# Attention values computed by channels and turned back, score maxima put into the queries by VectorE, decays by one scan: a chain of four transformer layers on one core

## The chip, the cores and the metric

The kernel runs on one core of a Trainium2 chip. The metric is the device time of one launch in microseconds. PE is the matmul engine (TensorE), PEld its weight loads, DVE is VectorE, ACT is ScalarE, POOL is GpSimd, SP is the engine whose queue issues all DMA here.

## The reference

Thirty-two sequences of 128 tokens with 256 channels each pass through four layers, all in float32. Layer 0 adds one attention with 16 heads, whose result is the same for all sequences here and is computed once. Layer 1 is a state space block (convolution over time, gate, decaying state) and a cross attention with 8 heads. Layer 2 holds two attentions with 16 heads of 16 channels, the first causal, and a feed-forward part. Layer 3 holds one causal attention with 16 heads and a feed-forward part of 1024 channels.

```python
A = -jnp.exp(A_log)
decay = jnp.exp(dt * A)
dbx = dt[..., None] * xh
def step(h, inp):
    dec, u, bt, ct = inp
    h = h * dec[:, :, None, None] + u[..., None] * bt[:, None, None, :]
    y = jnp.einsum('bhpn,bn->bhp', h, ct)
    return (h, y)
...
score = jax.nn.softmax(energy / jnp.sqrt(jnp.asarray(dk, energy.dtype)), axis=-1)
out = jnp.einsum('bhst,bhtk->bhsk', score, V) * m
```

The state space block is computed without the loop over time: for each of its 8 heads a 128x128 matrix holds the product of all decays between two times, it is multiplied by the inner products of B and C, and one matmul with `dbx` gives y.

## The kernel before, in words

The work of one sequence is cut into some 70 tasks (`xhatT`, `Q2`, `quads2`, ...), and up to four sequences are in work at a time. There is no scheduler at run time: the tables `TASKS`, `FIRST`, `LAST`, `SETUP` and `SHIFT` give each task of each sequence a place, one sequence is 14 units after the one before, and every engine runs its tasks in the order of these places (`ORDER`). `SHIFT` gives an engine an order of its own for some tasks. Engines wait for one another by semaphores alone, and each works through its list strictly in order, so a task that has to wait holds up all behind it. `SPARE` names tasks of the first sequences ahead of which PE runs matmuls that nobody reads.

Results of matmuls pass through a ring of four banks of PSUM (`RING_BANKS`). `claim` waits until the bank's last user has been read, `filled` waits for the bank to be full, `evacuated` for it to be read. Four more banks (`score`) hold the scores.

An attention `a_` with 16 heads (0, 2, 3 and 4; there are 97 of them, three for each sequence and one in the setup) goes through these tasks:

- `quads` (L698): the scores with queries on the partitions; in causal attentions `lay_causal` (L662) first lays the mask down.
- `scores` on DVE (`maxima`, L1252): the negated maximum of each query and head, written to `maxima_at`.
- `mT` on PE (`turn_maxima`, `flip`, L618): the maxima are turned by two transposes. On ACT (`shifts`, L1053) they are copied to `shift_rows` in two scalings, and POOL (`shift`, L1585) adds these to the queries QB. Each head has spare channels among its 32, in which the keys KE hold a one, so the maximum enters through the matmul itself.
- `quadsT` (L722): the same scores with keys on the partitions, already less the maximum. `exps` on ACT (L1042) takes the exponentials into `weights`.
- `values` (L765): for each head and each block of 32 queries one matmul, the exponentials as 128x32 weights and V2 (16 channels and a column of ones, 17 columns) moving: 64 matmuls, each of them two instructions in float32 and as many weight loads. The four blocks of queries go to four groups of 32 columns of the engine.
- `finish` on DVE (`weighted`, L1263 and L1264): division by the sum, then the layer norm (`moments`, L1222 to L1218, a root on POOL, L1512, and `normalise_affine`, L1233 and L1235).

The decays: POOL (`log_decays`, `am`, L1558) makes a matrix of 128x1024 from the logarithms, `ld` on PE (L839) sums it by two matmuls with the triangle `after`, 512 columns each, ACT (`decays`, L1115) takes two exponentials, and `decayed` on DVE (L1377) multiplies by the inner products. `Y` on PE (L849) uses the result, the gate on DVE (`Y`, L1386 and L1388) follows.

Other lines that matter: L1342 is the convolution on DVE, L1397 the addition of the state space block's output to the residual, L1413 that of the cross attention's output (`Wo`), L1047 a copy of 128x512 from PSUM on ACT in the attention with 8 heads.

## Time and profile before

| | |
|---|---|
| median of the runs shown | 1811.0 us (3 runs, 1804.14 to 1812.05) |
| profiled execution | 1813.73 us, span 1811.9 us |
| PE busy | 1655.2 us (91%), 33980 matmul instructions and as many weight loads |
| DVE busy | 1341.2 us (74%) |
| ACT busy | 1096.6 us (61%) |
| POOL busy | 687.1 us (38%) |
| granted clock of PE, mean | 0.982 |

The busy times come from one execution. They are shares of the whole span; what a task is worth depends on who waits for it at its place. "issue" as releaser means that the engine waited for nothing the profile shows.

### The profile page before, as it was taken

How to read it: one execution, taken by the hardware profiler on the slowest of the kernel's cores; microseconds unless marked ns; L12 is line 12 of the kernel's file. 1: busy time of each engine (PE TensorE's matmuls, PEld its weight loads, DVE VectorE, ACT ScalarE, POOL GpSimd, SP SyncE). 2: the span in 40 equal slices, each digit the busy share in tenths (PEclk: the TensorE clock that was granted, in tenths of full speed). 3: DMA queues.
4: the chain of work that ended last, by engine and by line, in shares of the span. 5: the costliest groups of instructions: out<-in, count | busy, mean ns of one | idle time of the engine just before them, and what ended most of it. 6: DMA issues, size and time to landing. Idle time of an engine off the chain costs nothing.

```text
span 1811.9 us, 78837 instructions
## 1 busy us (share of the span) xinstructions
PE 1655.2 (91%) x33980; PEld 1415.6 (78%) x33980; DVE 1341.2 (74%) x3357; ACT 1096.6 (61%) x2796; POOL 687.1 (38%) x1384
## 2 busy tenths in 40 slices
PE   6799989999999999999999999989999999999986
PEld 6678878787778777888787888877788777778765
DVE  4578867787867777867787877778777777787652
ACT  2456665575565665566565666656566656566653
POOL 2444433444423444433444433344333344443320
PEclk9999999999999999999999999999999999999998
DMA  7000000000000000000000000000000000000000
GB/s 262 12 6 3 11 14 12 11 3 11 9 14 11 12 3 11 12 12 12 11 3 11 12 12 11 12 6 9 11 12 12 12 12 3 12 9 5 6 3 10
DMA packets 26264, 28.71 MB, mean 16 GB/s; under 512 B 2240, under 2 KB 25024, under 8 KB 25792
## 3 DMA queue, kind: packets, MB, share of 16 engines
q1 hardware_dynamic: 25920, 23.67, 4.0%
q8 instruction: 271, 4.44, 1.0%
q14 instruction: 73, 0.60, 0.1%
HBM read 19.47 MB, written 4.19 MB: 13 GB/s over the span
## 4 chain that ended last, share of the span: by engine, by line
PE 71%; DVE 18%; issue 7%; ACT 2%; POOL 2%; DVEq 0%; DMA 0%; SPq 0%; POOLq 0%; ACTq 0%
PE ring L630 22%; PE ring L636 16%; PE ring L618 7%; PE ring L765 7%; DVE conv L1342 6%; PE score L698 6%; PE score L722 4%; PE ring L839 3%; PE score L662 2%; PE ring L849 2%; DVE maxima_at L1252 2%; DVE conv L1337 1%; PE ring L741 1%; POOL stat L1512 1%; PE score L678 1%
## 5 line engine op out<-in xcount | busy, mean ns | idle before, releaser
L1009 ACT COPY actT<-ring 128x256 f32<-128x256 f32 x256 | 94.4, 377 | 322.2 <-PE ring L618 322.1
L1252 DVE TENSOR_REDUCE maxima_at<-score 128x4 f32<-128x512 f32 x388 | 240.5, 681 | 56.3 <-PE score L698 56.2
L1512 POOL TENSOR_TENSOR stat<-stat 128x1 f32<-128x1 f32 x224 | 135.7, 610 | 376.7 <-DVE stat L1218 374.9
L1585 POOL TENSOR_TENSOR QB<-QB,shift_rows 128x512 f32<-128x512 f32 x97 | 124.5, 1283 | 288.5 <-ACT shift_rows L1053 288.4
L1042 ACT ACTIVATE weights<-score 128x512 f32<-128x512 f32 x388 | 200.3, 606 | 16.2 <-PE score L722 15.8
L1342 DVE SCALAR_TENSOR_TENSOR conv<-raw,vectors,conv 128x128 f32<-128x128 f32 x576 | 197.0, 397 | 6.8
L765 PE MATMUL ring<-V,weights 128*32 128x17 f32 x12416 | 131.4, 186 | 47.4 <-issue 46.0
L765 PEld LDWEIGHTS ring<-V,weights 128*32 128x32 f32 x12416 | 118.8, 110 | 62.9 <-issue 52.5
L630 PE MATMUL ring<-actT,w_q 128*128 128x128 f32 x1024 | 143.0, 282 | 10.8 <-issue 8.9
L630 PEld LDWEIGHTS ring<-actT,w_q 128*128 128x128 f32 x1024 | 124.9, 192 | 13.6 <-issue 8.4
L1526 POOL TENSOR_TENSOR dts<-dts,row_all 128x8 f32<-128x8 f32 x32 | 6.9, 216 | 323.7 <-ACT dts L1103 323.7
L630 PE MATMUL ring<-actT,w_up 128*128 128x128 f32 x1024 | 127.7, 278 | 0.5 <-ACT actT L1009 0.5
L722 PE MATMUL score<-QB,KE 32*128 32x128 f32 x3104 | 117.2, 287 | 5.7 <-POOL QB L1585 3.2
L630 PEld LDWEIGHTS ring<-actT,w_up 128*128 128x128 f32 x1024 | 119.3, 192 | 3.5 <-ACT actT L1009 0.7
L636 PE MATMUL ring<-w_down,gT 128*128 128x256 f32 x512 | 120.0, 388 | 2.1 <-issue 2.1
L722 PEld LDWEIGHTS score<-QB,KE 32*128 32x128 f32 x3104 | 98.0, 189 | 26.6 <-issue 19.4
L1235 DVE SCALAR_TENSOR_TENSOR res<-att,stat,row_all 128x256 f32<-128x256 f32 x128 | 75.0, 586 | 47.8 <-POOL stat L1512 46.3
L636 PEld LDWEIGHTS ring<-w_down,gT 128*128 128x128 f32 x512 | 97.5, 196 | 16.3 <-issue 3.6
L630 PE MATMUL ring<-cT,w_k 128*128 128x128 f32 x768 | 104.8, 279 | 0.0
L1233 DVE SCALAR_TENSOR_TENSOR att<-res,stat,row_all 128x256 f32<-128x256 f32 x128 | 102.5, 801 | 0.0
L630 PEld LDWEIGHTS ring<-cT,w_k 128*128 128x128 f32 x768 | 95.5, 191 | 5.5
L636 PE MATMUL ring<-w_v,cT 128*128 128x256 f32 x384 | 99.3, 381 | 0.3 <-issue 0.3
(174 smaller groups left out, 3955.2 us busy)
## 6 DMA issues: line engine op xcount, KB each, us to landing
cT<-in_ctxT SPq DMA_DIRECT2D x32, 128.0 KB, 2.3
x_in<-in_x SPq DMA_DIRECT2D x32, 128.0 KB, 2.3
out<-result SPq DMA_DIRECT2D x32, 128.0 KB, 1.7
row_all<-in_rows SPq DMA_DIRECT2D x1, 1420.0 KB, 9.9
w_in<-in_in_proj SPq DMA_DIRECT2D x1, 1288.0 KB, 7.1
w_k<-in_k SPq DMA_DIRECT2D x4, 256.0 KB, 6.6
w_v<-in_v SPq DMA_DIRECT2D x4, 256.0 KB, 6.3
w_q<-in_q SPq DMA_DIRECT2D x4, 256.0 KB, 7.3
```

The costliest lines, as they stand in the source:

```text
L618: last = nc.tensor.transpose(t[:, c * P:(c + 1) * P], src[:, c * P:(c + 1) * P], ident)
L630: last = mm(t[:, at:at + P], w[:, c, cols:cols + P], xT[:, c, :], start=(c == 0), stop=(c == n - 1))
L636: last = mm(t[:, at:at + hi - lo], xT[:, c, :], w[:, c, lo:hi], start=(c == 0), stop=(c == n - 1))
L698: last = mm(score[:, r, at:at + P], QB[rows_of, l, c, e, :], keys, start=(not masked and at == 0), stop=(c == DC - 1 and f == 1))
L722: last = mm(score[:, r, at:at + P], KE[rows_of, l, c, e, :], QB[rows_of, l, c, e, :], start=(not masked and at == 0), stop=(c == DC - 1 an ...
L765: last = mm(output[queries, h * (DH16 + 1):(h + 1) * (DH16 + 1)], weights[:, buffer, r, at + queries.start:at + queries.stop], V2[:, l, h, :],
L1042: run(weights[:, turned_buffer(it, a_, l), r, :], score[:, r, :], ACT.Exp).then_inc(S["exps"], 1)
L1233: step(stt(att[:, l, :], res[:, l, :], stat[:, l, 0:1], rows[g], ALU.subtract, ALU.mult))
L1252: nc.vector.tensor_reduce(maxima_at[:, maxima_buffer(it, a_, l), :, 32 * r:32 * r + 17:16], score[:, r, :].rearrange("p (c f k) -> p c f k ...
L1342: last = stt(conv[:, l % 2, c, :], raw[:, l % 2, c, k:k + P], conv_w[:, c, k:k + 1], conv[:, l % 2, c, :], ALU.mult, ALU.add)
L1512: tt(stat[:, l, 10:11], stat[:, l, 2:3], stat[:, l, 4:5], ALU.pow).then_inc(S[done], 1)
L1585: tt(QB[:, l, :, :, :], QB[:, l, :, :, :], shift_rows[:, :, :, :], ALU.add).then_inc(S[f"shift{a_}"], 1)
```

## The change

It does four things.

1. Values by channels. V2 is widened from 17 to 32 columns (the rest is zero) and becomes the weights, 128x32, one matmul for each head; the exponentials move, 128 queries at a time. The result has channels on the partitions. ACT copies it to `attT` (task `attT`), PE turns it back by four transposes (new task `back`, three more ring jobs for each sequence), and DVE reads `weighted` from the turned bank.
2. Maxima. `shift_rows`, ACT's scalings and POOL's addition go. DVE (`shifted`, in the task `mT`) multiplies the turned maxima in PSUM by `spare_row` and adds them to QB in two instructions.
3. Decays. POOL's 128x1024 product and the two matmuls go. PE turns the 128x8 logarithms (one transpose, one ring job instead of two), ACT takes the exponential of 8x127 into `rates_row`, SP writes these rows to DRAM (`ld`) and reads them back into all 128 partitions (`spread`, 4 KB each). DVE runs one `tensor_tensor_scan` over 128x1024 against `delta`, which holds the identity for each head, and `decayed` follows.
4. Orders. The tables of places are new for all engines, and so are the spare matmuls (113 instead of 63).

In the steady part the new order of PE is the following, with the number of the sequence relative to the one that enters; the old order differs from it by one to three places for most tasks and has no `back`, and DVE runs `scan` and `decayed` between `norm3` and `scores2`:

```
xhatT[0] Q1[-1] row[-2] xbc0[0] x3T[-2] mT4[-3] quads1[-1] K3[-2] Q3[-2] z1[0] xbc1[0] quads3[-2] turn1[-1] V3[-2] e3[-2] values1[-1]
n3[-2] quadsT4[-3] ctxT[-1] V1[0] Wo[-1] mT3[-2] z0[0] values4[-3] x2T[-1] ld[0] quadsT3[-2] pairs[0] back4[-3] K2[-1] values3[-2] Q2[-1]
back3[-2] K4[-2] V4[-2] x6T[-3] e2[-1] quads2[-1] V2[-1] x4T[-2] up0[-3] fc1[-2] Y[0] up1[-3] mT2[-1] fc2[-2] uT[0] quadsT2[-1] n2[-1]
proj[0] K1[0] x5T[-2] values2[-1] Q4[-2] xnT[0] back2[-1] down[-3] quads4[-2]
```

The core of the diff, the tables of places left out:

```diff
+def att_buffer(it, a_, l):
+
+    return it.number(TURNED_AT, a_, l) % ATT_BUFFERS
+
...
-        V2 = sb("V2", [P, G, H16, DH16 + 1])
+        V2 = sb("V2", [P, G, H16, P // TILES])
...
-        shift_rows = sb("shift_rows", [P, DC, 2, P])
+        attT = sb("attT", [P, ATT_BUFFERS, 4 * P])
...
+            def ld(it, l):
+                b, use = job(it, "ld", l)
+                sp.wait_ge(bank_read[b], use + 1)
+                sp.dma_start(rates_out[l % 2], rates_row[:, l % 2, :]).then_inc(S[f"rates_out{l % 2}"], 16)
+
+            def spread(it, l):
+                sp.wait_ge(S[f"rates_out{l % 2}"], nth_of_two(it, l) * 16)
+                sp.dma_start(decay[:, l % 2, :, :], rates_out[l % 2].partition_broadcast(P)).then_inc(S[f"decay_in{l % 2}"], 16)
+
...
-                pe.wait_ge(S[f"shift{a_}"], 1 if a_ == 0 else nth(it, l))
+                evacuated(it, f"mT{a_}", l)
...
                 buffer = turned_buffer(it, a_, l)
-                for c in range(DC):
+                for four in range(H16 // TILES):
                     for r in range(TILES):
-                        for e in range(2):
-                            h, at = 8 * c + 2 * r + e, (2 * c + e) * P
-                            for q, queries in enumerate(ROWS_OF):
-                                last = mm(output[queries, h * (DH16 + 1):(h + 1) * (DH16 + 1)],
-                                          weights[:, buffer, r, at + queries.start:at + queries.stop], V2[:, l, h, :],
-                                          start=True, stop=True)
-                                if h == H16 - 1:
-                                    last.then_inc(full if q == TILES - 1 else S[f"att_full{q}"], 1)
+                        h = TILES * four + r
+                        at = (2 * (h // 8) + h % 2) * P
+                        last = mm(output[ROWS_OF[r], four * P:(four + 1) * P], V2[:, l, h, :],
+                                  weights[:, buffer, h % 8 // 2, at:at + P], start=True, stop=True)
+                        if four == H16 // TILES - 1:
+                            last.then_inc(full if r == TILES - 1 else S[f"att_full{r}"], 1)
+
+            def back(it, a_, l):
+                evacuated(it, f"values{a_}", l, (f"back{a_}", l))
+                flip(it, f"back{a_}", l, attT[:, att_buffer(it, a_, l), :], 4)
 
             pe.wait_ge(S["const_in"], 16)
...
 
             def ld(it, l):
                 pe.wait_ge(S["am"], nth(it, l))
-                for half in range(2):
-                    t, full = claim(it, f"ld{half}", l)
-                    mm(t[:, :], after, decay[:, l % 2, 4 * half:4 * half + 4, :].rearrange("p h k -> p (h k)"),
-                       start=True, stop=True).then_inc(full, 1)
+                t, full = claim(it, "ld", l)
+                nc.tensor.transpose(t[0:MH, 0:P], dts[:, 5, l, :], ident).then_inc(full, 1)
...
 
-            def shifts(it, a_, l):
-
-                t, read = filled(it, f"mT{a_}", l)
-                for e in range(2):
-                    last = run(shift_rows[:, :, e, :], t[:, 0:D].rearrange("p (c k) -> p c k", c=DC), ACT.Copy,
-                               scale=spare_row[:, e:e + 1])
-                last.then_inc(read, 1)
+            def out_turned(it, a_, l):
+                for r in range(TILES - 1):
+                    act.wait_ge(S[f"att_full{r}"], nth_output(it, a_, l))
+                t, read = filled(it, f"values{a_}", l)
+                nc.scalar.copy(attT[:, att_buffer(it, a_, l), :], t[:, :]).then_inc(read, 1)
 
             def extended_keys(it, a_, l):
...
             def decays(it, l):
-                for half in range(2):
-                    t, read = filled(it, f"ld{half}", l)
-                    run(decay[:, l % 2, 4 * half:4 * half + 4, :].rearrange("p h k -> p (h k)"), t[:, :],
-                        ACT.Exp).then_inc(read, 1)
+                t, read = filled(it, "ld", l)
+                run(rates_row[:, l % 2, 1:], t[0:MH, 1:P], ACT.Exp).then_inc(read, 1)
 
             def Y(it, l):
...
+            def shifted(it, a_, l):
+
+                if a_ in (2, 3):
+                    dve.wait_ge(S[f"q{a_}_first"], nth(it, l))
+                t, read = filled(it, f"mT{a_}", l)
+                for e in range(2):
+                    last = stt(QB[:, l, :, e, :], t[:, 0:D].rearrange("p (c k) -> p c k", c=DC), spare_row[:, e:e + 1],
+                               QB[:, l, :, e, :], ALU.mult, ALU.add)
+                last.then_inc(read, 1)
+
             def weighted(it, a_, l, step, dst):
 
-                for r in range(TILES - 1):
-                    dve.wait_ge(S[f"att_full{r}"], nth_output(it, a_, l))
-                t, read = filled(it, f"values{a_}", l)
-                o = t[:, 0:H16 * (DH16 + 1)].rearrange("p (h e) -> p h e", h=H16)
+                t, read = filled(it, f"back{a_}", l)
+                o = t[:, :].rearrange("p (h e) -> p h e", h=H16)
                 step(nc.vector.reciprocal(rec[:, l, :], o[:, :, DH16]))
                 tt(dst.rearrange("p (h e) -> p h e", h=H16), o[:, :, 0:DH16],
                    rec[:, l, :].unsqueeze(2).broadcast_to((P, H16, DH16)), ALU.mult).then_inc(read, 1)
-                evacuated(it, f"values{a_}", l)
+                evacuated(it, f"back{a_}", l)
 
             def x1(it, l):
...
+            nc.vector.tensor_copy(delta[:, :].rearrange("p (h k) -> p h k", h=MH), ident.unsqueeze(1).broadcast_to((P, MH, P)))
+            nc.vector.memset(rates_row[:, :, :], 0.0)
             nc.vector.memset(maxima_at[:, :, :, :], 0.0).then_inc(S["ready_consts"], 1)
...
+                def scan(l):
+                    dve.wait_ge(S[f"decay_in{l % 2}"], nth_of_two(it, l) * 16)
+                    across = decay[:, l % 2, :, :].rearrange("p h k -> p (h k)")
+                    step(nc.vector.tensor_tensor_scan(across, across, delta[:, :], 0.0, ALU.mult, ALU.add))
+
                 def decayed(l):
-                    jobs = sorted(("CB", "ld1"), key=lambda what: place(it, what, l))
-                    for what in {job(it, what, l)[0]: what for what in jobs}.values():
-                        evacuated(it, what, l)
+                    evacuated(it, "CB", l)
                     tt(decay[:, l % 2, :, :], decay[:, l % 2, :, :],
                        state_gate[:, l % 2, :].unsqueeze(1).broadcast_to((P, MH, P)), ALU.mult).then_inc(S["M"], 1)
...
+            nc.gpsimd.memset(V2[:, :, :, DH16 + 1:], 0.0).then_inc(S["ones_col"], 1)
...
-                    step(tt(dts[:, 5, l, :], dts[:, 10, l, :], decay_rate, ALU.mult))
-                    tt(decay[:, l % 2, :, :], before.unsqueeze(1).broadcast_to((P, MH, P)),
-                       dts[:, 5, l, :].unsqueeze(2).broadcast_to((P, MH, P)), ALU.mult).then_inc(S["am"], 1)
+                    tt(dts[:, 5, l, :], dts[:, 10, l, :], decay_rate, ALU.mult).then_inc(S["am"], 1)
 
...
-
-                def shift(a_, l):
-
-                    evacuated(it, f"mT{a_}", l)
-                    tt(QB[:, l, :, :, :], QB[:, l, :, :, :], shift_rows[:, :, :, :], ALU.add).then_inc(S[f"shift{a_}"], 1)
 
                 def norm5(l):
```

## Rows read from the trace of the kernel before

**Rows 1.** The page: busy time and share, and the chain that ended last.

```profile
PE 1655.2 (91%) x33980; PEld 1415.6 (78%) x33980; DVE 1341.2 (74%) x3357; ACT 1096.6 (61%) x2796; POOL 687.1 (38%) x1384
...
PE 71%; DVE 18%; issue 7%; ACT 2%; POOL 2%; DVEq 0%; DMA 0%; SPq 0%; POOLq 0%; ACTq 0%
```

**Rows 2.** Stretch 200 to 1600 us: length, busy PE, PEld, DVE, ACT, POOL, clock, DMA share, GB/s.

```profile
200.00:1600.00 1400.00, 1305.99 (x27230) 1120.54 (x27229) 1081.37 (x2688) 878.89 (x2243) 556.87 (x1113) 0.99 0.04 10
```

**Rows 3.** Line 839: durations min/median/max, first and last start.

```profile
L839 PEld LDWEIGHTS ring<-decay,const x128: 186/190/338, 45.8 to 1681.7; 128*128 128x128 f32 x128
```

**Rows 4.** PE's waits from 200 to 1600 us: total, times, longest.

```profile
PE ring L765 <- issue: 34.1, 29, 2.1
PE ring L618 <- DVE res L1413: 19.0, 23, 0.9
...
PE ring L636 <- issue: 1.1, 2, 0.8
```

**Rows 5.** Timeline of PE: start, length, what, idle before.

```profile
812.99 1.25 PE L765 MATMUL ring<-V,weights 128*32 128x17 f32 x127
815.40 0.18 PE L765 MATMUL ring<-V,weights 128*32 128x17 f32 x1 [1.16 <-issue]
...
816.73 0.60 PE L618 MATMUL ring<-const,conv 128*128 128x128 f32 x4
817.16 1.06 PE L630 MATMUL ring<-actT,w_k 128*128 128x128 f32 x8
...
823.20 1.88 PE L839 MATMUL ring<-decay,const 128*128 128x512 f32 x4
824.92 1.03 PE L636 MATMUL ring<-w_v,cT 128*128 128x256 f32 x4
...
829.63 1.10 PE L849 MATMUL ring<-dbx,decay 128*32 128x64 f32 x64
...
834.42 1.17 PE L722 MATMUL score<-QB,KE 32*128 32x128 f32 x32
...
838.83 1.27 PE L765 MATMUL ring<-V,weights 128*32 128x17 f32 x128
840.03 1.16 PE L630 MATMUL ring<-actT,w_q 128*128 128x128 f32 x8
```

**Rows 6.** The page: PE's instruction queue and two DMA issues, us to landing.

```profile
q8 instruction: 271, 4.44, 1.0%
...
x_in<-in_x SPq DMA_DIRECT2D x32, 128.0 KB, 2.3
...
row_all<-in_rows SPq DMA_DIRECT2D x1, 1420.0 KB, 9.9
```

**Rows 7.** Groups by shape: busy us, mean ns, idle before.

```profile
L1585 POOL TENSOR_TENSOR QB<-QB,shift_rows 128x512 f32<-128x512 f32 x97 | 124.5, 1283 | 288.5 <-ACT shift_rows L1053 288.4
...
L1233 DVE SCALAR_TENSOR_TENSOR att<-res,stat,row_all 128x256 f32<-128x256 f32 x128 | 102.5, 801 | 0.0
...
L1377 DVE TENSOR_TENSOR decay<-decay,state_gate 128x1024 f32<-128x1024 f32 x32 | 38.7, 1210 | 2.7 <-ACT decay L1115 2.6
...
L1047 ACT COPY weights<-ring 128x512 f32<-128x512 f32 x64 | 34.4, 590 | 19.5 <-PE ring L618 19.5
...
L1397 DVE SCALAR_TENSOR_TENSOR res<-ring,stat,res 128x256 f32<-128x256 f32 x32 | 15.5, 484 | 13.3 <-PE ring L636 11.2 <-POOL stat L1512 1.2
```

**Rows 8.** Lines 1233 and 1388: duration ns min/median/max.

```profile
L1233 DVE SCALAR_TENSOR_TENSOR att<-res,stat,row_all x128: 473/476/2054, 94.0 to 1796.2; 128x256 f32<-128x256 f32 x128
...
L1388 DVE TENSOR_TENSOR zs<-tz,zs x32: 691/1030/1540, 52.2 to 1689.1; 128x512 f32<-128x512 f32 x32
```

**Rows 9.** Timeline of DVE and of POOL at the decays' product.

```profile
819.06 2.05 DVE L1233 SCALAR_TENSOR_TENSOR att<-res,stat,row_all 128x256 f32<-128x256 f32 x1
...
818.94 1.90 POOL L1558 TENSOR_TENSOR decay<-const,dts 128x1024 f32<-128x1024 f32 x1
```

**Rows 10.** DVE's waits from 200 to 1600 us.

```profile
DVE res L1235 <- POOL stat L1512: 37.4, 73, 0.9
```

More of the change, by code:

```diff
@@ L224 @@
 MAXIMA_BUFFERS = 2
+ATT_BUFFERS = 2
 RING_BANKS = 4
@@ L347 @@
 down norm3; norm5 x1r"""
[L348 to L352 removed]
+NEXT_BUT_ONE = "Y ld; pairs xbc0; proj z1; Y z1; Y pairs; uT pairs; Y dt; decayed pairs; down up0; store down; x1 loadx; proj xbc0; uT xbc0"
+DVE_ALONE = ("finish2 norm2 finish3 norm3 norm4 finish4 norm5 x1 x1r xhat spread scan decayed conv0 conv1 silu loadx loadc").split()
 def in_time(chains, later):
```

352 lines of the change are left out of this document (171 added, 181 removed).

## Prediction

> **What bounds the kernel now.** I read the page first, then the stretches, one line's first and last start, PE's waits, two pieces of the timeline, and the groups by shape. PE is busy 91% of the span, DVE 74%, ACT 61%, POOL 38%; the chain that ended last runs 71% on PE, 18% on DVE and 7% through "issue", time in which the engine waited for nothing the profile shows [rows 1]. The clock is at its upper level (2.4 GHz) nearly throughout, granted 0.99 from 200 to 1600 us [rows 2], so everything is costed at that level. The decay matmuls start first at 45.8 and last at 1681.7 us [rows 3]; 31 steps lie between, so one sequence takes 52.8 us. The 1400 us from 200 to 1600 hold 26.5 sequences: PE busy 1305.99/26.5 = 49.2 us each, DVE 1081.37/26.5 = 40.8 us [rows 2].
>
> What PE waits for there is the main reading. Seven "issue" rows, from 34.1 down to 1.1 us, add to 71.6 us (2.7 us a sequence); the rows with DVE as releaser, nearly all of it the 19.0 us behind Wo, to 20.9 us (0.8 us) [rows 4]. With the 1306.0 us busy that fills the 1400. The largest issue row belongs to the value products, and the stall sits inside them: 1.16 us after 127 of 128 instructions [rows 5]. `values` waits at its start only, so no semaphore can stop it there. It puts out 128 matmul instructions with 128 weight loads in 1.20 us (838.83 to 840.03 [rows 5]), while PE's instruction queue brought 4.44 MB in 271 packets [rows 6], 16.4 KB each: one for some 251 of PE's 67,960 matmuls and weight loads. I take the stalls for instructions that come too late where PE uses up a whole packet in about 1.2 us.
>
> **The change, part by part, for one sequence.**
>
> Decays on PE. Removed: four instructions of 512 columns, 823.20 to 824.92 = 1.72 us. Added: one transpose, 0.43/4 = 0.11 us (four took 816.73 to 817.16) [rows 5]. Together -1.61 us.
>
> Values, three times. Before 1.20 us each; a row of the timeline is 0.07 longer than the distance to the next start, since it holds the tail of its last matmul (1.27 against 1.20), and I take that off the others. After: 32 matmul instructions in 8 rounds of four side by side, 128 columns each. No row shows 128x32 weights with 128 columns. A round of four takes 37.5 ns at 17 columns (1.20 us/32) and 64 ns at 64 (L849, 1.03 us/16 [rows 5]); along that slope 128 columns give 100 ns. Weights of 32 rows and 128 columns with the same 128 columns moving take 137 ns (L722, 1.10 us/8 [rows 5]). So 0.80 to 1.10 us; nearer the rows with the same weights, I take 0.95: -0.25 each, -0.75 us.
>
> Turning back, three times four transposes at 0.43 us: +1.29 us. PE work in all: 49.2 - 1.61 - 0.75 + 1.29 = 48.1 us (47.7 to 48.6).
>
> Stalls. A value product falls from 128 to 32 matmul instructions, and no other group of PE's puts out so many so fast: L849 has 64 in 1.03 us [rows 5]. I leave 0.2 of the 2.7 us: -2.5 us (0 to -2.7). One page speaks against this step. The Trainium skill, "Runtime: NRT & Kernel Launch", section "Instruction fetch mechanics", says that an engine's instruction memory is refilled in 16 KiB blocks while the current one is executed, and that this is mostly hidden. By that rule the 2.7 us have another cause and may stay. The packet size in this trace agrees with the page; a stall in the middle of a group without a wait doesn't agree with "hidden".
>
> DVE. Added: six updates of QB. The nearest row is L1397, also a scalar_tensor_tensor of 128x256 with one input in PSUM, 484 ns [rows 7]: 2.9 us. Added: one scan of 128x1024. No row shows a scan. Below stands one pass over as much, L1377, 1.21 us [rows 7]; above, two such passes, one for the multiply and one for the add, 2.42 us. I take 2.4, since each element needs the one before it. The Trainium skill, "DVE: opcode table, instruction layouts, handler registers and perf-mode slots", section "Datapath and trigger behaviour", says that this scan runs at half throughput; from the length of L1377 that would be 2.4 us too, and no run here shows it yet.
>
> DVE also gets time back. L1233 takes 476 ns in the median but 801 on average, up to 2054 [rows 7, 8]: at 819.06 it lasted 2.05 us beside POOL's product for the decays (818.94, 1.90 us [rows 9]). The excess is 128 x 0.325 = 41.6 us; that of L1388, median over minimum, 32 x 0.34 = 11 us [rows 8]. Both large partners on POOL go: that product and the update of QB (L1585, 1.28 us, 97 times [rows 7]). With some 8 us at the convolution, an estimate, 61 us or 1.9 us a sequence; bounds 0 and 2.5. DVE then: 40.8 + 2.9 + 2.4 - 1.9 = 44.2 us.
>
> ACT loses two exponentials and six scalings and gains three copies of 128x512 at 0.59 us (L1047 [rows 7]) and one small exponential; at 878.89/26.5 = 33 us [rows 2] it has room. The copy lies behind `values`; `back` comes one or two tasks later, about 1 us of PE work, so only tenths show. Ahead of the transposed scores, two ACT scalings and 1.28 us of POOL become 2 x 0.48 us on DVE, but in DVE's queue: in front of `mT3` there stands half a convolution, in front of `mT2` the state space layer's gate. `quadsT` waits for it, and behind `quadsT` all of PE.
>
> The trip through DRAM. In the new order eleven PE tasks from quadsT3 to e2 stand between `ld` and where DVE comes to the scan, by their rows' lengths 7.6 us. The trip is an exponential (0.3, an estimate), a write and a spread of 512 KB; the rows are 2.3 us for 128 KB and, for a broadcast, 9.9 us for 1420 KB while all weights shared the queues [rows 6]. With 2 and 3 us the trip is 5.3 us: hidden. On SP's queue `spread` stands behind loadc of the next sequence, an old store and a loadx; what these wait for ended a period earlier, and they cost their issue.
>
> How DVE and PE meet. DVE needs its 44.2 us, the POOL roots and ACT sums it waits for (37.4 us in the largest row [rows 10], with two smaller ones 67.3 us, 2.5 a sequence) and some 1.4 of small gaps: 48.1 us, as much as PE. Scan and `decayed` (3.6 us) lie between `norm3` and `Y`, while PE has up0 and fc1 (3.1 us); then comes the gate, then `mT2`. I expect half a microsecond there and 1.0 elsewhere: PE's waits for DVE go from 0.8 to 2.2 us (0.8 to 4).
>
> Sum: 48.1 + 0.2 + 2.2 = 50.5 against 52.8, -2.3 us, times 31 = -71. Start: the trip and the scan less POOL's product, +4. End: no stalls, but two turns back, -2. The order of tasks is otherwise nearly the old one. In all -69: span 1811.9 to 1743. The profiled run took 1813.7, 1.8 more than its span and 0.15% over the median of 1811.0 of the runs shown; 1743 + 1.8 = 1744.8, less 0.15%: 1742. I say 1740.
>
> **Rivals.**
> - The stalls stay: what stops PE isn't the value products' own pace. They would then hide DVE's waits: 48.1 + 2.7 + 0.8 = 51.6, -1.2 x 31 = -37, with start and end 1776. For it speaks that under half of the issue time carries the value products' line; against it, where they stand. The rule of the skill's page above leads here.
> - DVE becomes the bound. Today it idles 12.0 us a sequence, 8 of them for PE; if half of that can't be taken out of two interlocked queues, 48.1 + 4.0 = 52.1: -0.7 x 31 = -22, 1791. For it speaks that both engines now need 48.1 us.
> - All goes in, DVE's waits stay 0.8 and no stall is left: 48.9, -3.9 x 31 = -121, 1692.
> - Slower: the spread is late. At 9.9 us, and 2.3 for the write, the trip is 12.5 us against 7.6 of cover; 4.9 us a sequence stop DVE at the scan, with scores2, Y and mT2 queued behind: 48.1 + 0.2 + 0.8 + 4.9 = 54.0, +1.2 x 31 = +37, about 1850. It decides from a trip of 7.6 + 3.6 = 11.2 us. Against it: in the steady stretch the DMA engines are busy 4% [rows 2].
>
> That the change does nothing is no case: instructions fall away.
>
> **Numbers.** Chances: the forecast 0.50 (its own range 1712 to 1768), stalls stay 0.12, DVE bound 0.17, all in 0.13, spread late 0.06, something not seen 0.02. The range 1700 to 1792 leaves out the last two and half of "all in" and of little else. Half a per cent, 9 us, is about what a measurement of this kernel can tell from no change. Faster 0.88, same 0.04 (the upper edge of the DVE case), slower 0.08.
>
> **What the changed profile would show.** Value products: 3104 matmul instructions, 0.95 x 97 = 92 us of PE and under 110 busy; issue rows of 200 to 1600 us under 10 us (near 70, and the first rival is right). L1233's counterpart at a mean near 480 ns, DVE at 83% of its span, the scan at 1.2 to 2.4 us. A wait of DVE for the spread in the steady stretch would be the last rival. PE's waits for DVE near 2 us a sequence, at the transposed scores and at Y; each microsecond more or less there moves the time by 31, and that is what would make the prediction wrong first.

## The result: 1672 us, faster than forecast

The changed kernel takes 1672.27 us (median of 4 runs, 1670.92 to 1675.6) against 1808.24 us (4 runs on the same chip). The ratio is 0.9251, 95% interval [0.9223, 0.9279]. I had forecast 1740 with a range of 1700 to 1792: the sign is right, the size is not, and the time lies below the range, beyond even the rival "all goes in" (1692).

The page of the changed kernel: busy times, the chain that ended last by engine, PE's instruction queue, and the new transfer through DRAM (KB each, us to landing). They answer to [rows 1, 6].

```profile
PE 1616.5 (97%) x25060; PEld 1393.2 (83%) x25060; DVE 1387.1 (83%) x3585; ACT 1039.8 (62%) x2667; POOL 493.3 (29%) x1256
...
PE 55%; DVE 36%; issue 5%; POOL 2%; DMA 1%; ACT 1%; SPq 0%; DVEq 0%; POOLq 0%; ACTq 0%
...
q8 instruction: 202, 3.31, 0.8%
...
decay<-rates_out SPq DMA_DIRECT2D x32, 512.0 KB, 3.9
```

PE is busy 97% of the span in place of 91%, and DVE's share of the chain has doubled: both engines are now close to the whole period. The stretch 200 to 1500 us (columns as in [rows 2]), the line of the Y products with its first and last start (durations in ns first), and the three largest of PE's five waits in that stretch (total us, times, longest):

```profile
200.00:1500.00 1300.00, 1291.56 (x20548) 1118.15 (x20547) 1140.52 (x2944) 856.64 (x2201) 408.82 (x1042) 1.00 0.07 21
```

```profile
L858 PE MATMUL ring<-dbx,decay x2048: 216/219/243, 50.3 to 1546.7; 128*32 128x64 f32 x187
```

```profile
PE ring L858 <- DVE decay L1396: 3.9, 22, 0.4
PE ring L843 <- DVE conv L1364: 1.2, 4, 0.4
PE ring L849 <- POOL dts L1578: 0.5, 2, 0.3
```

Y starts 31 steps apart from first to last: (1546.7 - 50.3)/31 = 48.27 us for a sequence, where [rows 3] gave 52.8. I use this period for every kernel below. The 1300 us hold 1300/48.27 = 26.9 sequences. PE is busy 1291.56/26.9 = 48.0 us in each and idle 0.31 (8.4 us in 1300), of which the three rows above and the two others, 0.5 and 0.3 us, make 6.4. In the stretch no "issue" row of PE is left, where [rows 4] had 34.1 us at one line and 71.6 in all (in 1400 us). DVE is busy 1140.52/26.9 = 42.35 us.

Two pieces of PE's timeline (start, length, what, idle before):

```profile
810.30 1.10 PE L858 MATMUL ring<-dbx,decay 128*32 128x64 f32 x64 [0.16 <-DVE decay L1396]
...
819.36 1.08 PE L773 MATMUL ring<-weights,V 128*32 128x128 f32 x32
820.37 1.16 PE L639 MATMUL ring<-actT,w_q 128*128 128x128 f32 x8
```

The value products take 820.37 - 819.36 = 1.01 us without a gap, against 1.20 plus stalls in [rows 5]. Y, which I took for a place where PE waits, waits 0.16 us. The groups by shape that answer to [rows 7, 8], and the new ones (busy us, mean ns, idle before):

```profile
L1358 DVE SCALAR_TENSOR_TENSOR conv<-raw,vectors,conv 128x128 f32<-128x128 f32 x576 | 169.0, 349 | 6.8
L1269 DVE SCALAR_TENSOR_TENSOR QB<-ring,const,QB 128x256 f32<-128x256 f32 x194 | 84.5, 477 | 20.4 <-PE ring L627 20.3
L1392 DVE TENSOR_TENSOR_SCAN decay<-decay,delta 128x1024 f32<-128x1024 f32 x32 | 73.1, 2284 | 3.0 <-DMA decay<-rates_out 3.0
...
L1241 DVE SCALAR_TENSOR_TENSOR res<-att,stat,row_all 128x256 f32<-128x256 f32 x128 | 62.3, 487 | 39.6 <-POOL stat L1533 36.3 <-DVE att L1239 0.4
L1239 DVE SCALAR_TENSOR_TENSOR att<-res,stat,row_all 128x256 f32<-128x256 f32 x128 | 60.9, 476 | 0.0
...
L1407 DVE TENSOR_TENSOR zs<-tz,zs 128x512 f32<-128x512 f32 x32 | 22.1, 692 | 1.1
```

L1239 is the old L1233: 476 ns on average, not 801. L1407 is the old L1388: 692, not 1056. DVE waits 3.0 us in the whole run for the spread row, so the trip through DRAM is hidden.

### The profile page after: what moved, and what is told of

The parts are those of the page before. It is cut to its first block, busy times and chain, and to the rows that moved or that the text cites. A ratio compares the mean times of both kernels' runs of the same rounds, so it can differ in the third digit from the quotient of the medians.

```text
span 1673.8 us, 61139 instructions
## 1 busy us (share of the span) xinstructions
PE 1616.5 (97%) x25060; PEld 1393.2 (83%) x25060; DVE 1387.1 (83%) x3585; ACT 1039.8 (62%) x2667; POOL 493.3 (29%) x1256
## 4 chain that ended last, share of the span: by engine, by line
PE 55%; DVE 36%; issue 5%; POOL 2%; DMA 1%; ACT 1%; SPq 0%; DVEq 0%; POOLq 0%; ACTq 0%
PE ring L639 18%; PE ring L645 14%; PE ring L627 6%; DVE conv L1358 5%; DVE maxima_at L1258 5%; PE score L707 4%; DVE decay L1392 4%; PE score L731 3%; PE ring L773 3%; DVE decay L1396 2%; PE ring L858 2%; DVE conv L1364 2%; DVE QB L1269 2%; DVE conv L1353 2%; PE score L671 2%
## 5 line engine op out<-in xcount | busy, mean ns | idle before, releaser
L1533 POOL TENSOR_TENSOR stat<-stat 128x1 f32<-128x1 f32 x224 | 131.7, 594 | 617.2 <-DVE stat L1224 616.6
L1358 DVE SCALAR_TENSOR_TENSOR conv<-raw,vectors,conv 128x128 f32<-128x128 f32 x576 | 169.0, 349 | 6.8
L1184 ACT ACTIVATE gT<-ring,vectors 128x128 f32<-128x128 f32 x256 | 73.0, 368 | 72.2 <-PE ring L639 71.5
L645 PE MATMUL ring<-w_down,gT 128*128 128x256 f32 x512 | 115.9, 379 | 1.3 <-issue 1.3
L773 PE MATMUL ring<-weights,V 128*32 128x128 f32 x3104 | 106.9, 278 | 3.4 <-issue 3.3
L1269 DVE SCALAR_TENSOR_TENSOR QB<-ring,const,QB 128x256 f32<-128x256 f32 x194 | 84.5, 477 | 20.4 <-PE ring L627 20.3
L1063 ACT COPY attT<-ring 128x512 f32<-128x512 f32 x97 | 56.2, 579 | 72.7 <-PE ring L773 72.6
L773 PEld LDWEIGHTS ring<-weights,V 128*32 128x32 f32 x3104 | 80.5, 111 | 23.8 <-issue 10.1
L639 PE MATMUL ring<-actT,w_in 128*128 128x128 f32 x768 | 98.7, 279 | 0.7 <-DVE q_bias L1337 0.7
```

Source lines behind the costliest of these rows:

```text
L639: last = mm(t[:, at:at + P], w[:, c, cols:cols + P], xT[:, c, :], start=(c == 0), stop=(c == n - 1))
L645: last = mm(t[:, at:at + hi - lo], xT[:, c, :], w[:, c, lo:hi], start=(c == 0), stop=(c == n - 1))
L773: last = mm(output[ROWS_OF[r], four * P:(four + 1) * P], V2[:, l, h, :], weights[:, buffer, h % 8 // 2, at:at + P], start=True, stop=True)
L1184: last = run(gT[:, l % 2, c, :], t[:, k * P:(k + 1) * P], ACT.Gelu, bias=up_b[:, c:c + 1])
L1269: last = stt(QB[:, l, :, e, :], t[:, 0:D].rearrange("p (c k) -> p c k", c=DC), spare_row[:, e:e + 1], QB[:, l, :, e, :], ALU.mult, ALU.add)
L1358: last = stt(conv[:, l % 2, c, :], raw[:, l % 2, c, k:k + P], conv_w[:, c, k:k + 1], conv[:, l % 2, c, :], ALU.mult, ALU.add)
```

## Experiments

All twelve have the kernel before beside them on the same chip; its median moved between 1807 and 1819 us. The changed kernel was measured only for the result, where the kernel before had 1808, so a difference from its 1672 us can be off by some us, by about 10 in run 12. Line numbers shift by a few lines between the kernels.

**1 and 2. Computation and order apart.** The change does two things at once: it computes three parts otherwise, and it has new orders of tasks for all engines. The first kernel has the old computation under the new orders, the second the new computation under the old ones. Tasks that the borrowed order doesn't have were put in by hand, next to their producers.

```diff
 the first (the second has it the other way round, with the new computation):
-    K1=-101.6778, K2=-85.3719, K3=-77.8105, K4=-66.1055, KE2=-53.2043, KE3=-34.7422, Q1=-92.624, Q2=-86.0387, Q3=-77.5392,
+    K1=27.1941, K2=36.4796, K3=45.2686, K4=51.2561, KE2=36.4927, KE3=55.6023, Q1=30.3419, Q2=36.7225, Q3=45.6768, Q4=56.4087,
...
```

> All three parts of the computation as before (values by queries, maxima through ACT and POOL, decays by POOL's product and two matmuls), under the new orders; finish4 a little earlier on DVE, and the last exps4 a little later on ACT, so that nothing blocks. Instruction theory (the stalls of PE come from the value products' 128 matmul instructions, the rest of the gain from less work): the orders alone are worth little, 1780 to 1815 us, and the issue rows of PE from 200 to 1500 us stay above 50 us. Rival, the orders made the gain: below 1750 us and the issue rows under 20 us.

> The changed computation under the old tables of places; the new tasks get places next to their neighbours (back half a unit to one unit after values, scan just ahead of decayed). Theory that DVE has slack once its collisions with POOL and PE's stalls are gone: one sequence takes 48.5 to 49.5 us, 1680 to 1715 us in all. Rival, as I had forecast: DVE and PE block each other at 48 us of need each and only a tuned order avoids it: 50.5 us and more a sequence, 1740 us and above, with PE's waits for DVE above 2 us a sequence.

Measured: 2033.86 us (ratio 1.1274 [1.1204, 1.1344]) and 2094.68 us (1.1577 [1.1534, 1.1619]). The first is far from both expectations, in its "issue" rows too (33.9 us from 200 to 1500, where the theory wanted over 50 and the rival under 20); the second lies on the rival's side and far beyond its figure. PE's largest waits from 200 to 1600 us, of the first:

```profile
PE score L669 <- POOL QB L1592: 95.0, 24, 4.0
PE ring L846 <- POOL decay L1565: 28.1, 16, 2.4
PE ring L772 <- issue: 26.5, 29, 2.4
```

and of the second:

```profile
PE ring L644 <- DVE V L1482: 75.1, 16, 5.7
PE ring L632 <- ACT attT L1068: 36.7, 46, 3.5
PE ring L632 <- DVE res L1437: 26.3, 19, 1.4
```

What is to be seen: in the first, PE stands 4 us at the transposed scores in each sequence until POOL has added the shift to the queries; with these tasks placed as they are, the new order leaves no room for ScalarE's copies and that addition. In the second, PE waits for results that DVE makes in time in the order meant for it. PE's busy time for the same instructions grew too: 52.3 us a sequence against 49.3 in the kernel before, and 52.0 against 48.0 in the changed one; the granted clock of the stretch is 0.94 in both runs, against 0.99 and 1.00. An order and a computation belong together, and neither half can be read as the share of its part. The hand-placed tasks are untuned, so the 224 and 285 us above the kernel before say only that much.

**3. The value products alone put back** (queries on the rows of the result, 128 matmul instructions of 17 columns, no turning back):

```diff
-                        last = mm(output[ROWS_OF[r], four * P:(four + 1) * P], V2[:, l, h, :],
-                                  weights[:, buffer, h % 8 // 2, at:at + P], start=True, stop=True)
+                            for q, queries in enumerate(ROWS_OF):
+                                last = mm(output[queries, h * (DH16 + 1):(h + 1) * (DH16 + 1)],
+                                          weights[:, buffer, r, at + queries.start:at + queries.stop], V2[:, l, h, 0:DH16 + 1],
+                                          start=True, stop=True)
```

> The changed kernel with only the value products as before: 128 matmul instructions each of 17 columns, no copy to attT, no turning back (finish4 a little earlier on DVE). PE's work falls by 3 x (1.01 + 0.44 - 1.20) = 0.75 us a sequence. Instruction theory: the stalls come back, 2 to 2.7 us a sequence, inside or just behind the value products, which gives 1710 to 1735 us. Rival, the stalls had another cause (order, ring of banks, ACT): no stalls, 47.5 us a sequence, about 1650 us.

Measured: 1801.77 us (0.9963 [0.9939, 0.9987]), period (1670.5 - 49.6)/31 = 52.3 us, 4.0 more than the changed kernel's. PE's waits from 200 to 1600 us:

```profile
PE ring L840 <- DVE conv L1355: 40.6, 19, 3.2
PE ring L773 <- issue: 22.2, 13, 2.6
PE score L730 <- issue: 9.6, 8, 1.9
```

The "issue" rows are back (38 us in all), at the value products and at work behind them. A wait for DVE that the changed kernel hardly has (1.2 us) is now the largest. The time is far above the expected 1710 to 1735 us, and not because of the stalls: the "issue" rows make 1.4 us a sequence, less than the 2 to 2.7 expected. PE's waits for DVE make 1.8 us, 1.6 more than in the changed kernel, and its busy time is 49.0 us a sequence instead of the 47.2 that the work alone would give; the granted clock is 0.96 against 1.00.

**4. Instruction supply by itself.** PE alone, no waits: 24 times 64 products of 17 columns, 32 of 64, 16 of 128, and 64 of 17 again (its last part is as the first). Each product is two matmul instructions in the trace, with a weight load each. It computes nothing of the reference.

```
for bank, (count, columns) in enumerate(((64, 17), (32, 64), (16, 128), (64, 17))):
    for _ in range(24):
        for n in range(count):
            q = slice(32 * (n % 4), 32 * (n % 4) + 32)
            last = mm(ring[bank][q, 0:columns], w[:, q], w[:, 0:columns], start=True, stop=True)
```

> PE alone, no waits, zero operands; the output is zeros and nothing of the reference is computed. 24 times each: 128 matmul instructions of 17 columns (as the value products before), 64 of 64 columns (as Y), 32 of 128 columns (as the value products after), then the first again. Instruction theory: the first and the last part can't hold 1.20 us a product; they run on average at 1.6 us or more with pauses that name no releaser, the part with 32 instructions holds about 1.0 us without pauses. Rival, supply is no limit: all parts hold 1.20, 1.03 and 1.0 us a product without pauses.

One run, span 257.5 us. PE's timeline, two pieces of the first part and one of the third:

```profile
9.74 1.91 PE L42 MATMUL ring<-w 128*32 128x17 f32 x128 [1.55 <-issue]
...
13.20 1.91 PE L42 MATMUL ring<-w 128*32 128x17 f32 x128 [1.55 <-issue]
...
135.96 10.68 PE L42 MATMUL ring<-w 128*32 128x128 f32 x384 [0.46 <-issue]
```

Exactly 128 matmul instructions with their 128 weight loads, then a pause with no releaser, and again: the next 128 start 3.45 to 4.0 us after the last. Nothing in the kernel could hold them up. The page has PE's instruction queue at 65 packets for 16,896 matmuls and weight loads, one for 260. With 64 columns the pauses are still there (0.5 to 2.0 us). With 128 columns, 384 matmul instructions take 10.68 us, 3.6 for 128, and the pauses all but vanish. So the instruction theory holds: in this kernel PE gets 256 instructions in about 3.6 us and no faster. The granted clock was 1.00 from 9 to 90 us and 0.50 from 180 to 250, and lots, lengths and pauses are the same in both. A lot of the first part takes 1.91 us where the full kernel needs 1.20; why is not shown, but one lot of 17 columns right behind the part with 128 took 1.26 us, and the next still started 3.73 us after it.

**5 and 6. The maxima alone, the decays alone put back,** under the orders of the changed kernel (with places given by hand to the tasks that come back).

```diff
-                    last = stt(QB[:, l, :, e, :], t[:, 0:D].rearrange("p (c k) -> p c k", c=DC), spare_row[:, e:e + 1],
-                               QB[:, l, :, e, :], ALU.mult, ALU.add)
+                    last = run(shift_rows[:, :, e, :], t[:, 0:D].rearrange("p (c k) -> p c k", c=DC), ACT.Copy,
+                               scale=spare_row[:, e:e + 1])
...
+                    tt(QB[:, l, :, :, :], QB[:, l, :, :, :], shift_rows[:, :, :, :], ALU.add).then_inc(S[f"shift{a_}"], 1)
```

```diff
-                nc.tensor.transpose(t[0:MH, 0:P], dts[:, 5, l, :], ident).then_inc(full, 1)
+                    mm(t[:, :], after, decay[:, l % 2, 4 * half:4 * half + 4, :].rearrange("p h k -> p (h k)"),
+                       start=True, stop=True).then_inc(full, 1)
...
-                    step(nc.vector.tensor_tensor_scan(across, across, delta[:, :], 0.0, ALU.mult, ALU.add))
...
+                    tt(decay[:, l % 2, :, :], before.unsqueeze(1).broadcast_to((P, MH, P)),
+                       dts[:, 5, l, :].unsqueeze(2).broadcast_to((P, MH, P)), ALU.mult).then_inc(S["am"], 1)
```

> The changed kernel, with the maxima alone put back: ScalarE makes the scaled copies of mT, GpSimd adds them to the queries, VectorE does none of it. Per sequence VectorE loses about 2.9 us of work, GpSimd gets about 5, ScalarE about 2.6, TensorE's work is the same. Theory A (VectorE's load was what I priced wrongly; PE waits when VectorE is full): the time stays at 1672 or falls a little, 1660 to 1680. Theory B (what counts is how long the results are under way in an order that leaves them little room: two engines in place of one between mT and quadsT): PE waits for GpSimd's addition, some 2 to 3.5 us in each sequence as in the first run, 1730 to 1790.

> The changed kernel, with the decays alone put back: GpSimd multiplies, two products of 512 columns, ScalarE's exponential over 1024 columns; no scan, no way through DRAM. TensorE gets 1.6 us more for each sequence, VectorE loses the scan of 2.3. Theory A (work alone, since PE is busy 97% of the span and VectorE gets freer): 1672 + 32 x 1.6 = 1724, 1710 to 1735. Theory B (the way from the decay rate to Y is a chain of its own, and the product on GpSimd comes late in this order, as the 28.1 us in the first run): 1745 to 1790.

Measured: 1940.65 us (1.0719 [1.0676, 1.0763]) with a period of 56.5 us, and 1810.68 us (0.9992 [0.9965, 1.0018]) with one of 52.5. PE's waits from 200 to 1500 us, of the maxima's run and of the decays':

```profile
PE score L672 <- POOL QB L1603: 87.1, 22, 4.0
PE score L732 <- POOL QB L1603: 23.9, 23, 2.5
```

```profile
PE ring L848 <- POOL decay L1576: 40.7, 22, 2.3
```

In both runs DVE has less to do than in the changed kernel (40.3 and 41.7 us a sequence), and the time is longer: theory B of both, but beyond its 1790, by 21 us with the decays and by 151 with the maxima. Per sequence PE waits 111/23.0 = 4.8 us for POOL's addition there. PE's busy time grows too, to 1172.09/23.0 = 51.0 us from 48.0, for the same instructions; the granted clock of the stretch is 0.94 against 1.00, after waits of up to 4 us. With the decays, the period is 4.3 us longer: PE idles 1.6 us more, and its busy time is 2.7 us longer, not the 1.6 expected (the matmuls of 512 columns took 762 ns on average, 645 in the kernel before). The decays' run also shows in its groups and its timelines what DVE and POOL do to each other:

```profile
L1364 DVE SCALAR_TENSOR_TENSOR conv<-raw,conv 128x768 f32<-128x768 f32 x25 | 59.0, 2359 | 0.9
```

```profile
808.76 2.44 DVE L1364 SCALAR_TENSOR_TENSOR conv<-raw,conv 128x768 f32<-128x768 f32 x1
```

```profile
808.50 1.90 POOL L1576 TENSOR_TENSOR decay<-const,dts 128x1024 f32<-128x1024 f32 x1
```

The silu product takes 2359 ns on average beside POOL's product, and 1135 over the same stretch of the changed kernel. It began 0.26 us after POOL's and ended 0.80 us after POOL's end (808.76 + 2.44 against 808.50 + 1.90): most of it was done only when POOL had finished. The Trainium skill, "SBUF — State Buffer", section "SBUF: two separate sides", says that a VectorE instruction with two SBUF inputs and a GpSimd one that reads SBUF exclude each other for the whole instruction. The trace agrees nearly: by that rule it would have waited POOL's remaining 1.64 us and then taken its own 1.14, 2.8 us in all, and it took 2.44.

**7 and 8. What a microsecond of DVE costs.** The changed kernel with dummy reductions: two of 128x1024 behind the scan, or four of 128x512 at K1, both halves of the convolution, and the scan.

```diff
                     step(nc.vector.tensor_tensor_scan(across, across, delta[:, :], 0.0, ALU.mult, ALU.add))
+                    for j in range(2):
+                        step(nc.vector.tensor_reduce(spill[:, 0:1], across, AX_X, ALU.max))
```

> The changed kernel with two more VectorE reductions over 128x1024 behind each scan, whose result nobody reads: about 2.4 us more for each sequence, 42.4 + 2.4 = 44.8, a little over the 44.2 that I had forecast for VectorE, and that on the way from the scan to Y. Theory A (PE's waits go by VectorE's load): the 2.2 us of waits that I forecast come back, 1672 + 60 = 1730, 1715 to 1745. Theory C (VectorE's 5.9 us of idle time in each sequence takes it): at most 1685. If the place counts and not the load, PE's wait for the decays L1396 grows to some 2 us in each sequence, 1720 to 1750.

> The changed kernel with four more VectorE reductions over 128x512 for each sequence, one behind K1, one behind each half of the convolution and one behind the scan, whose result nobody reads: about 2.5 us more, as much as in the run before this one, but in four places. Theory A (load): the same as there, 1715 to 1745. Theory C (slack): at most 1685. The place counts: clearly less than there, 1680 to 1705.

Measured: 1768.44 us (0.9783 [0.9732, 0.9833]), period (1637.5 - 50.8)/31 = 51.2, and 1739.23 us (0.9609 [0.9572, 0.9647]), period (1613.0 - 51.2)/31 = 50.4. The added groups' rows, of the first and of the second:

```profile
L1395 DVE TENSOR_REDUCE spill<-decay 128x1 f32<-128x1024 f32 x50 | 61.0, 1220 | 1.7
```

```profile
L1363 DVE TENSOR_REDUCE spill<-delta 128x1 f32<-128x512 bf16 x52 | 35.1, 676 | 0.0
L1396 DVE TENSOR_REDUCE spill<-delta 128x1 f32<-128x512 bf16 x25 | 17.2, 686 | 0.9
L1349 DVE TENSOR_REDUCE spill<-delta 128x1 f32<-128x512 bf16 x25 | 16.9, 676 | 0.0
```

and PE's waits:

```profile
PE ring L859 <- DVE decay L1399: 63.5, 24, 2.8
```

```profile
PE ring L859 <- DVE decay L1400: 21.0, 24, 1.2
PE ring L628 <- DVE res L1436: 16.1, 22, 1.1
PE ring L917 <- DVE nonzero L1446: 14.7, 26, 1.1
PE ring L844 <- DVE conv L1367: 7.2, 21, 0.7
```

At the scan, 2 x 1.22 = 2.44 us make the period 2.9 longer; in four places, 2.7 us make it 2.1 longer. DVE has 5.9 us idle in each sequence of the changed kernel, and little of it takes the work. Theory C is out; run 8 lies in theory A's range, run 7 lies 23 us above it. The idle time is in small pieces (at most 0.8 us each in the timeline of one period that I read, mostly at POOL's roots and at PE's transposes), and each piece is there because the next input isn't; that this is why work put in front of it is not made up is my reading of these rows. The place changes the price from 0.8 to 1.2 us of time for a microsecond of DVE.

**9 and 12. The old instruction count in the new form.** Each value product of 128 columns is cut into four of 32, with the same result: 128 matmul instructions and 128 weight loads for a layer. In run 9 four neighbours write the same group of 32 rows, from the same weights loaded anew; in run 12 (the loop over `part` outside the one over `r`) they go round the four groups.

```diff
-                        last = mm(output[ROWS_OF[r], four * P:(four + 1) * P], V2[:, l, h, :],
-                                  weights[:, buffer, h % 8 // 2, at:at + P], start=True, stop=True)
+                        for part in range(4):
+                            last = mm(output[ROWS_OF[r], four * P + part * 32:four * P + part * 32 + 32], V2[:, l, h, :],
+                                      weights[:, buffer, h % 8 // 2, at + part * 32:at + part * 32 + 32], start=True, stop=True)
```

> The changed kernel, computing the same, with each value product of 128 columns cut into four of 32 over the same weights: 128 products with 128 weight loads for a layer of attention instead of 32 and 32, which is the instruction count of the old value products; columns, results and all the rest as they are. Instruction theory (the old stalls came from the count alone): pauses without a releaser come back on TensorE, some 2.5 us in each sequence, and 0.2 us more work for a layer, 0.6 in a sequence: 1672 + 32 x 3.1 = 1771, and some more where the order knocks on, 1745 to 1800. Rival (the stalls came from something else in the old form, its narrow writes or who read them): no pauses, only the work, 1675 to 1700.

> As the run with the value products in quarters, but the four quarters go round the four groups of 32 rows of the result, one after the other, as the old value products did; in the run before four neighbours wrote the same group, and a layer's 128 products took 2.7 us in place of the 1.2 that I had counted on. 128 products of 33 columns that go round took 13 ns each in the trace of before (19.8 us for 1536), so 1.65 us for a layer here, 0.6 more than the changed kernel's, 1.9 in a sequence: 1672 + 61 = 1733. Instruction theory: pauses without a releaser on TensorE again, more than the 1.4 us for each sequence of the run before since the products go faster, 2 to 3 us, so 1800 to 1840. Rival: no pauses worth naming, 1725 to 1750.

Measured: 1887.68 us (1.0436 [1.0402, 1.0469]), period 54.5, and 1820.34 us (1.0019 [0.9988, 1.0051]), period (1685.7 - 51.9)/31 = 52.7. The timeline of PE, of run 9:

```profile
825.39 2.74 PE L774 MATMUL ring<-weights,V 128*32 128x32 f32 x128
828.06 0.44 PE L627 MATMUL ring<-const,res 128*128 128x128 f32 x2
```

and of run 12, and under it run 12's waits of PE from 200 to 1500 us:

```profile
837.99 1.13 PE L774 MATMUL ring<-weights,V 128*32 128x32 f32 x108
841.10 0.38 PE L774 MATMUL ring<-weights,V 128*32 128x32 f32 x20 [1.99 <-issue]
...
864.79 1.30 PE L774 MATMUL ring<-weights,V 128*32 128x32 f32 x128
866.02 0.44 PE L627 MATMUL ring<-const,res 128*128 128x128 f32 x2
```

```profile
PE ring L774 <- issue: 48.1, 20, 3.7
PE ring L639 <- issue: 9.5, 5, 3.0
PE score L731 <- issue: 5.2, 6, 1.2
PE ring L627 <- issue: 3.8, 4, 2.4
```

Run 12 does a layer's values in 1.23 us (864.79 to 866.02), nearly the 1.20 of the old form, and the pauses are back in the middle of a group, as in [rows 5]: 66.8 us in 1300/52.7 = 24.7 sequences, 2.7 us in each, the very figure of before. Order of tasks, data and columns are the changed kernel's; only the products were cut into more instructions. The period is 4.4 us longer: 2.5 us are idle time, 0.7 the value products (3 x 0.22), and the other 1.3 are busy time of PE outside them, at a granted clock of 0.98 against 1.00. The time falls into the expected range partly by luck, since the products were much faster than the 1.65 us that I had put. Run 9's products are slower (2.67 us a layer), and its pauses smaller, 1.4 us a sequence (34.1 us of such rows in 23.8 sequences): the slower PE went through its instructions, the less it waited for them. My expectation for run 9 had the work wrong, 0.2 us more for a layer where it was 1.66: I had not reckoned with what four neighbours in one group of rows cost. Whether it is the shared group of rows or the shared weights that makes them slower, these two runs don't separate.

**10. DVE without the scan.** The spread row goes into the gate as it is, so the decays are not computed.

```diff
-                    step(nc.vector.tensor_tensor_scan(across, across, delta[:, :], 0.0, ALU.mult, ALU.add))
```

> The changed kernel without the scan of the decays (the spread row goes into the gate as it is, so its output isn't the reference's): VectorE loses 2.28 us for each sequence, 42.4 to 40.1, all else the same. If VectorE's load goes on deciding below where it stands, as it did when I added to it (27 to 39 us for each us in a sequence), 1672 - 60 = 1610. If TensorE alone is the bound now (it waits 0.31 us in a sequence), no more than these waits: 1660 to 1672.

Measured: 1661.78 us (0.9193 [0.9167, 0.922]), period (1535.5 - 46.3)/31 = 48.04. DVE's 2.28 us less are worth 0.23 us of the period, less than the 0.31 that PE had been idle; the first Y comes 4.0 us earlier. PE is busy 1294.12 of the 1300 us, so from here on it sets the time.

**11. More for POOL.** Two products of 128x512 from two SBUF inputs behind the decay rate; nobody reads them.

```diff
+                    for j in range(2):
+                        step(tt(spill[:, :, :], ident.unsqueeze(1).broadcast_to((P, 4, P)),
+                                gate_mask.unsqueeze(1).broadcast_to((P, 4, P)), ALU.mult))
```

> The changed kernel with two more GpSimd products of 128x512 from two inputs behind the decay rate, whose result nobody reads: about 2.5 us more for each sequence on an engine that is busy 29% of the span. If only VectorE's own load counts: 1672 to 1680. If GpSimd's work slows VectorE's instructions beside it (in the run with the decays put back, the silu product took 2.36 us instead of 1.14 beside GpSimd's): 1 to 1.3 us more on VectorE in a sequence, and at 27 to 39 us for each us, 1700 to 1725; the rows of VectorE's silu or convolution are then longer.

Measured: 1719.09 us (0.9508 [0.9475, 0.954]), period (1591.5 - 51.7)/31 = 49.7, 1.4 more. DVE's groups by shape over the span, and under them two waits from 200 to 1500 us:

```profile
L1240 DVE SCALAR_TENSOR_TENSOR att<-res,stat,row_all 128x256 f32<-128x256 f32 x128 | 85.6, 669 | 0.0
...
L1365 DVE SCALAR_TENSOR_TENSOR conv<-raw,conv 128x768 f32<-128x768 f32 x32 | 53.6, 1674 | 5.4 <-ACT raw L1119 4.3
```

```profile
PE ring L844 <- DVE conv L1365: 17.5, 26, 0.9
```

```profile
DVE res L1242 <- POOL stat L1534: 27.8, 54, 0.7
```

Not one instruction was added to DVE, but its busy time grew: by 85.6 - 60.9 = 24.7 us at the norm, 53.6 - 36.4 = 17.2 at the silu (36.4 in the changed kernel) and 4.1 at the convolution, 46.0 us, 1.4 a sequence. The period grew by the same 1.4. A busier POOL could also have delayed its results; DVE's largest wait for it didn't grow (27.8 us, 28.0 in the changed kernel), and PE's waits for it are 0.2 us a sequence.

## Why the prediction was right and wrong

**Right: PE's work.** 48.1 us forecast, 48.0 measured. Inside it the values took 1.01 us a layer where I had 0.95 in a range of 0.80 to 1.10, and a turn back takes 0.44 (821.58 to 822.02) where I had 0.43. With these the sum would be 48.3; the granted clock of the stretch, 1.00 against 0.99, may be the rest.

**Right: the stalls are instructions that come late.** 0.2 us forecast to be left, none seen. Runs 4, 9 and 12 show it apart from the rest: with nothing but more instructions for the same columns, 2.7 us a sequence come back. The first rival (the stalls stay) is out. The Trainium skill, "Runtime: NRT & Kernel Launch", section "Instruction fetch mechanics", has the cost of a new block of instructions "mostly hidden"; run 4's pauses of 1.5 us and more decide against it for products as short as these.

**Right: the trip through DRAM is hidden,** at 3.0 us of waiting in the whole run, and the scan at 2284 ns is near the 2.4 us taken. Start and end moved little, as forecast: the first Y comes at 50.3 us against 49.9, and behind the last one there are 127.1 us (1673.8 - 1546.7) against 124.2, together +3.3 where I had +2.

**Wrong: "PE's waits for DVE go from 0.8 to 2.2 us (0.8 to 4)".** They fell to 0.22 us (5.9 in the stretch), and PE's whole idle time is 0.31 us a sequence, where the sum had 2.4 (2.2 and 0.2 of stalls). That is 2.1 us a sequence, 65 of the 68 us by which the forecast missed. It rests on two faults.

The first is a size. I had DVE at 44.2 us, and it is 42.35. Its time given back was forecast as 1.9 us with an upper bound of 2.5, and it was (41.6 + 28.0 + 12.7 + 11.7 + 6.9 - 5.6)/32 = 3.0 us: the norm's product and the gate's about as counted, the convolution 28.0 us (197.0 to 169.0 over the span) where I had put 8 as an estimate, the norm's second instruction 12.7 that I had left out, two residual updates 6.9, and 5.6 lost at the silu. The updates of the queries (84.5/32 = 2.6 us) and the scan were 0.4 too dear; of the 1.85 us between 44.2 and 42.35 that leaves 0.35. It is of the size of an error in the way of adding: a busy time counts moments in which two records overlap once, and I added lengths of records to it. All of DVE's groups add to 1399.7 us in the kernel before, where the page has it busy 1341.2, and to 1461.7 in the changed one, where it has 1387.1; the overlap grew by 16.1 us, 0.5 a sequence. Collisions were also in the means of four groups that I had not looked at or had put too low (the convolution, the norm's second instruction, two residual updates); I had looked for them in the two most conspicuous rows. What such an error weighs is shown by runs 7, 8 and 11: a microsecond more on DVE costs 0.8 to 1.2 of the period here. The 1.85 us that I had too many are so, as an estimate, 1.4 to 2.2 us of period, which is the size of the miss. At the load that I had forecast, the kernel would by these prices have taken some 1717 to 1740 us; run 8, with DVE busy 44.9 us a sequence, took 1739, and run 7, with 44.8, took 1768.

The second is a rule: I added DVE's work, its waits for POOL and small gaps to 48.1 us, saw that it equals PE's work, and charged PE half a microsecond at Y and 1.0 elsewhere. The sum has room for that only if the orders make the two collide. I had also written that "the order of tasks is otherwise nearly the old one". Runs 1 and 2 show that order and computation have to fit each other: with either half alone PE waits 4 us and more at a place. A trace of the kernel before can't show how well an order of another kernel fits, and my range (its lower edge at 0.8 us of waits) didn't allow for waits below the old ones. How much of the 0.6 us below the old 0.8 comes from the order and how much from fewer stalls knocking on, as in run 3, is not settled.

**The parts.** Put back one at a time, values, maxima and decays cost 130, 268 and 138 us; all three together 362, less than their sum. The figures hold for this order, with the returning tasks placed by hand, and are no shares of the gain of 136. The DVE rival was wrong in its figure, 4.0 us of idle time of PE where there are 0.31, but right that DVE is near being the bound: runs 7 and 8 cross the edge, and the change stops just short of it. Run 10 shows the other side: 2.3 us less on DVE gain 10 us. No kernel here beats the changed one with the whole computation; with PE busy 97% of the span, what is left to gain lies in PE's own work.

## What to carry to other kernels

Count the instructions, not only the columns: a group of products that goes through 256 of PE's instructions in about 1.2 us can stop in the middle, because here they came in about 3.6; fewer and wider products took the stall away. When GpSimd loses instructions that read SBUF, look at the mean against the median of every VectorE group with inputs there, not of the worst two alone. And where two engines are both near the period, measure the price of a microsecond on the second one with a dummy instruction before trusting its idle time: here 5.9 us of idle time took at most 0.6 of 2.7 us, and 2.3 us less were worth a tenth of their length.

## What the runs showed of the hardware that I had not expected

- In run 4 PE's instructions come in lots of 256: 128 matmul instructions of 17 columns and 128 weight loads, then a pause of 1.5 to 2.1 us, a period of 3.45 to 4.0 us, at a granted clock of 1.00 and of 0.50 alike. At 128 columns the lot takes 3.6 us of work and the pauses all but go (0.2 to 0.5 us).
- 128 matmul instructions of 32 columns take 1.23 us when four neighbours write four groups of 32 rows in turn (run 12), and 2.67 us when they write the same group from the same weights (run 9).
- A VectorE instruction beside a GpSimd one, both with two SBUF inputs: 2359 ns instead of 1135 (run 6). GpSimd's may suffer as well: in run 11 the dummy product took 1543 ns on average, and the gate's of the same size 1273; these are two different products.
- A scan of 128x1024 takes 2284 ns, where a multiplication of the same size takes 1225.
